# A four-layer gated cross-attention kernel: query projections two head groups at a time, with the bias added by TensorE

## The reference, cut to what matters

```python
x = x + tanh(g_xattn[l]) * xattn_l(layernorm(x), ctx)     # l = 0..3
x = x + tanh(g_ffn[l])   * ffn_l(layernorm(x))
# layer 0 and 2 (16 heads of 8): q = x@Wq + bq; k = ctx@Wk + bk; v = ctx@Wv + bv
#   out = softmax(q k^T * scale [+ mask * -1e9]) v @ Wo + bo   (mask in layer 2 only)
# layer 1 (16 heads of 8): q = x@Wq.T; k, v of concat(ctx, x) (64 + 256 keys), no biases;
#   the first key has weight tanh(gate), the softmax goes over the rest; layernorm of the result, @ Wp.T + bp
# layer 3 (8 heads of 64): plain cross-attention, then the output projection
```

## Time and profile before

| | us |
|---|---|
| median of 3 runs (lowest, highest) | 1292.36 (1283.95, 1293.24) |
| the profiled execution, whole | 1285.64 |
| its span, first to last instruction | 1283.9 |
| mean granted TensorE clock in it | 0.842 of full speed |
| busy: TensorE matmul, VectorE, ScalarE, GpSimd | 977.4, 771.4, 571.7, 393.6 |
| first DMA issue of attention 0, 1, 2, 3 | 16.82, 213.59, 815.74, 1016.87 |
| statistics' first operation of feed-forward 1, 2 (L1457) | 537.2, 957.5 |
| first DMA issue of feed-forward 0, 3 | 126.40, 1163.94 |

### The profile page before, as it was taken

The page is one execution under the profiler, slowest core; times in us unless marked ns, Lnnn a source line. Parts: engine busy times, 40 slices in busy tenths (PEclk is TensorE's granted clock), DMA queues, the critical chain, the costliest instruction groups (busy, mean ns, idle before and its releaser), DMA issues. The chain is left out here.

```text
span 1283.9 us, 17163 instructions
## 1 busy us (share of the span) xinstructions
PE 977.4 (76%) x5366; PEld 731.0 (57%) x5366; DVE 771.4 (60%) x1924; ACT 571.7 (45%) x1101; POOL 393.6 (31%) x519
## 2 busy tenths in 40 slices
PE   2797576698888888488888888478867578883766
PEld 2575354566566665266666666357745357772544
DVE  3687565566766777366666656356765414545674
ACT  1575242355555555155555544156634133321553
POOL 2432002122323232146565656333310132210321
PEclk9899677667777778689999999689978679996887
DMA  4000000000000000000000000100000200000001
GB/s 117 1 2 2 1 1 19 1 18 18 18 18 18 18 9 10 1 1 1 1 1 1 1 1 1 36 1 2 2 19 1 64 2 1 1 1 1 1 1 33
DMA packets 25607, 14.12 MB, mean 11 GB/s; under 512 B 10776, under 2 KB 25007, under 8 KB 25391
## 3 DMA queue, kind: packets, MB, share of 16 engines
q1 hardware_dynamic: 25518, 13.03, 3.8%
HBM read 11.98 MB, written 1.05 MB: 10 GB/s over the span
## 5 line engine op out<-in xcount | busy, mean ns | idle before, releaser
L1470 POOL TENSOR_TENSOR L1f_h<-L1f_h,L1f_gb 128x512 f32<-128x512 f32 (+1 forms) x96 | 152.2, 1588 | 116.5 <-DVE L1f_h L1760 96.7
L718 ACT ACTIVATE L_pt<-bank 128x512 f32<-128x512 f32 x224 | 131.3, 597 | 60.8 <-PE bank L604 56.9
L705 ACT ACTIVATE L_part<-bank,L_bias_ca,const 128x256 fp32r<-128x256 f32 x128 | 68.9, 563 | 111.9 <-PE bank L545 111.9
L406 POOL TENSOR_TENSOR L_kc<-L_kc_all,const 128x256 fp32r<-128x256 f32 x96 | 59.0, 618 | 179.7 <-PE bank L604 127.1
L1760 DVE TENSOR_TENSOR L1f_h<-L1f_a,bank 128x512 f32<-128x512 f32 (+1 forms) x96 | 65.4, 682 | 69.9 <-ACT L1f_a L1600 69.3
L1600 ACT ACTIVATE L1f_a<-bank 128x512 f32<-128x512 f32 (+1 forms) x96 | 57.3, 597 | 111.9 <-PE bank L1525 111.8
L1768 DVE TENSOR_TENSOR L1f_h_lo<-L1f_h,L1f_h_hi 128x512 fp32r<-128x512 f32 (+1 forms) x96 | 88.2, 919 | 11.1 <-ACT L1f_h_hi L1613 11.1
L844 DVE TENSOR_REDUCE L_ms<-bank 128x2 f32<-128x512 f32 x128 | 84.5, 687 | 17.0 <-PE bank L566 16.7
L566 PE MATMUL bank<-L_k,L_q 32*128 32x256 f32 x256 | 73.4, 397 | 12.2 <-DVE L_ms L844 8.9
L830 DVE SCALAR_TENSOR_TENSOR L_q<-bank,L_bias_c,L_part 128x256 fp32r<-128x256 f32 x96 | 46.2, 481 | 58.9 <-ACT L_part L705 57.7
L842 DVE TENSOR_REDUCE L_mc<-bank 128x8 f32<-128x512 f32 (+1 forms) x96 | 65.4, 682 | 24.2 <-PE bank L559 14.8
(11 more groups left out here) (405 smaller groups left out, 2608.9 us busy)
## 6 DMA issues: line engine op xcount, KB each, us to landing
L_raw<-in_L_ffn_w_dram SPq DMA_DIRECT2D x8, 176.0 KB, 2.3
L_raw<-in_L_ffn_v_dram SPq DMA_DIRECT2D x8, 176.0 KB, 2.5
const<-in_const_dram SPq DMA_DIRECT2D x1, 1036.0 KB, 5.0
x<-in_x_dram SPq DMA_DIRECT2D x2, 512.0 KB
L_raw<-in_L_ffn_w_dram SPq DMA_DIRECT2D x8, 128.0 KB, 2.6
L_mask<-in_mask_Bx1xSxS_ff_dram SPq DMA_DIRECT2D x2, 512.0 KB
out_dram<-x SPq DMA_DIRECT2D x2, 512.0 KB
L_raw<-in_L_ffn_w_dram SPq DMA_DIRECT2D x8, 48.0 KB, 2.5
```

What stands on the lines that cost most here:

```text
L705: last = act.activation(part[:, i].bitcast(F32R), b_proj[:, i * S:(i + 1) * S], ACT.Identity, bias=bias_ca[:, i, g:g + 1], scale=pr.c("ak" ...
L718: act.activation(pt[:, g // 2, (g % 2) * NS + i], b_st[(g * NS + i) % 2][:], ACT.Exp, scale=scale).then_inc(sem["exp_done"], 1)
L1470: pool.tensor_tensor(h[0:m, r], h[0:m, r], gb[0:m, gate_slot(c)], ALU.mult).then_inc(sem["h_done"], 1)
```

## The change

Six things are changed.

1. In layers 0 and 2 two groups are projected in one pass ("unit"): `proj(b, u)` makes groups 2u and 2u+1 in the two halves of one 512-column bank; there are two units per batch. ScalarE rounds 512 columns at once (Copy with a scale operand and no bias), VectorE adds 512 columns at once (tensor_tensor). In layer 1 a unit is q and k of one group, rounded by two ScalarE operations (k's scale differs, `ak1`), and added by one of VectorE.
2. The bias is added by TensorE, as the first matmul of each half: in layers 0 and 2 over two rows (`bias_q`, the rounded bias and its rest; `ones_r`), in layer 1 over one row (`neg_row`) and for k only.
3. q and k lie in one tile `qk`: in layers 0 and 2 a ring of three pairs, in layer 1 four pairs (q, k).
4. In `order`, layers 0 and 2 have a `proj` in groups 1 and 3 only, for batch b+1.
5. The bias preparation: `bias_row` and `bias_x` have two partitions, VectorE makes `bias_part` and `bias_q`, TensorE turns only the key bias (four matmuls in the code, not eight).
6. Only the first 409 columns of the constants are loaded at the start. `selc` is loaded by the attentions 0 and 2, `sum3` and `self3` by attention 3, `self0` and `self3` by the feed-forwards 0 and 3, each into a buffer that is free then, ahead of the wait for the stage's loads.

```diff
-                  ("selc", 256), ("i2", 128), ("self0", 512), ("self3", 512), ("e8", 8),
-                  ("sum3", 512)):
+                  ("ak1", 1), ("neg_row", 128), ("i2", 128), ("e8", 8),
+                  ("selc", 256), ("self0", 512), ("self3", 512), ("sum3", 512)):
...
+KEPT = CONST["selc"][0]
...
-                sp.dma_start(pr.const[:], ins["const"]).then_inc(const_in, 16)
+                sp.dma_start(pr.const[:], ins["const"][:, 0:KEPT]).then_inc(const_in, 16)
...
-        part = sb("part", [P, 2, S])
-        q = sb("q", [P, NG, S], F32R)
+        part = sb("part", [P, 2 * S])
+        qk = sb("qk", [P, NG if own_keys else 3, 2, S], F32R)
...
+        UNITS = NG if own_keys else NG // 2
+        def unit(b, g):
+            return b * UNITS + (g if own_keys else g // 2)
+        def query(b, g):
+            return (g, 0) if own_keys else (unit(b, g) % 3, g % 2)
...
-            + [s for g in (0, 1) for s in (("proj", 0, g), ("keys", 0, g))] + banks("scores", 0, 0) + [("proj", 0, 2), ("keys", 0, 2)] \
+            + [("proj", 0, u) for u in range(UNITS // 2)] + [("keys", 0, 0), ("keys", 0, 1)] + banks("scores", 0, 0) \
+            + [("proj", 0, UNITS // 2), ("keys", 0, 2)] \
...
-                for at in group(g + 3):
-                    steps += [("proj", *at), ("keys", *at)]
+                if own_keys:
+                    steps += [("proj", *at) for at in group(g + 3)]
+                elif more and g % 2:
+                    steps += [("proj", b + 1, g // 2)]
+                steps += [("keys", *at) for at in group(g + 3)]
...
+                if not gated:
+                    sp.dma_start(pt[:, 0, 0, 0:2 * P], pr.late_const("selc")).then_inc(sem["loaded"], 16)
...
-                def proj(b, g):
+                def proj(b, u):
                     pe.wait_ge(sem["xt_lo"], b + 1)
-                    need(pe, sem["qk_split"], b * NG + g)
-                    cols = slice(g * P, (g + 1) * P)
-                    for i in range(2 if own_keys else 1):
-                        o = b_proj[:, i * S:(i + 1) * S]
-                        pe.matmul(o, wx[:, 2 * i, cols], xt_hi[:], start=True, stop=False)
+                    need(pe, sem["qk_split"], b * UNITS + u)
+                    for e in range(2):
+                        g, i = (u, e) if own_keys else (2 * u + e, 0)
+                        cols = slice(g * P, (g + 1) * P)
+                        o = b_proj[:, e * S:(e + 1) * S]
+                        if biased:
+                            pe.matmul(o, bias_q[:, cols], ones_r[:], start=True, stop=False)
+                        elif i == 1:
+                            pe.matmul(o, neg_row[:], ones_r[0:1], start=True, stop=False)
+                        alone = not (biased or i == 1)
+                        pe.matmul(o, wx[:, 2 * i, cols], xt_hi[:], start=alone, stop=False)
                         pe.matmul(o, wx[:, 2 * i, cols], xt_lo[:], start=False, stop=False)
                         last = pe.matmul(o, wx[:, 2 * i + 1, cols], xt_hi[:], start=False, stop=True)
...
-                def proj(b, g):
-                    act.wait_ge(sem["proj_done"], b * NG + g + 1)
-                    need(act, sem["qk_split"], b * NG + g)
-                    for i in range(2 if own_keys else 1):
-                        last = act.activation(part[:, i].bitcast(F32R), b_proj[:, i * S:(i + 1) * S], ACT.Identity,
-                                              bias=bias_ca[:, i, g:g + 1], scale=pr.c("ak" if i else "aq"))
+                def proj(b, u):
+                    act.wait_ge(sem["proj_done"], b * UNITS + u + 1)
+                    need(act, sem["qk_split"], b * UNITS + u)
+                    if own_keys:
+                        act.activation(part[:, 0:S].bitcast(F32R), b_proj[:, 0:S], ACT.Copy, scale=pr.c("aq"))
+                        act.activation(part[:, S:].bitcast(F32R), b_proj[:, S:], ACT.Copy, scale=pr.c("ak1")).then_inc(sem["proj_hi"], 1)
+                    else:
+                        act.activation(part[:].bitcast(F32R), b_proj[:], ACT.Copy, scale=pr.c("aq")).then_inc(sem["proj_hi"], 1)
...
-                    for i in range(2 if own_keys else 1):
-                        last = dve.scalar_tensor_tensor((k if i else q)[:, g], b_proj[:, i * S:(i + 1) * S], bias_c[:, i, g:g + 1],
-                                                        part[:, i], ALU.add, ALU.add)
+                    need(dve, sem["st_done"], b * U + (u + 1) * NS - U if own_keys else (2 * b + u - 2) * 2 * NS)
+                    at_u = u if own_keys else (2 * b + u) % 3
+                    dve.tensor_tensor(qk[:, at_u].rearrange("p e s -> p (e s)"), b_proj[:], part[:], ALU.add).then_inc(sem["qk_split"], 1)
...
+                    prep(dve.tensor_scalar(bias_part[:].bitcast(F32R), bias_x[:, 0], pr.c("am")[0:2], None, ALU.mult))
+                    prep(dve.tensor_tensor(bias_q[:], bias_x[:, 0], bias_part[:], ALU.add))
...
+                sp.dma_start(sum3[:].rearrange("p c n -> p (c n)"), pr.late_const("sum3")).then_inc(sem["loaded"], 16)
+                sp.dma_start(pt[:, 0:2].rearrange("p c s -> p (c s)"), pr.late_const("self3")).then_inc(sem["loaded"], 16)
...
+                if layer in (0, 3):
+                    sp.dma_start(h[:, 0], pr.late_const(f"self{layer}")).then_inc(sem["loaded"], 16)
```

More of the change, by code:

```diff
@@ L484, in _ @@
                 if biased:
[L486 to L490, removed]
+                    pe.wait_ge(sem["prep_dve"], 6)
+                    for g in range(NG):
+                        last = pe.matmul(b_sc[1][:, g:g + 1], bias_x[0:1, 1, g * P:(g + 1) * P], ones1[0:1, 0:1],
+                                         start=True, stop=True)
                     last.then_inc(sem["prep_pe"], 1)
                 pe.wait_ge(sem["prep_dve"], DVE_WEIGHTS)
-                for g, bank in enumerate((b_st[0], b_st[1], b_mt, b_o)):
+                for g, bank in enumerate(KV):
                     cols = slice(g * P, (g + 1) * P)
@@ L558, in scores @@
                             ts = slice(t * P, (t + 1) * P)
-                            last = pe.matmul(o[:, t * S:(t + 1) * S], q[:, g, ts], kc[:, g], start=True, stop=not masked)
+                            last = pe.matmul(o[:, t * S:(t + 1) * S], qk[:, at_q, e_q, ts], kc[:, g], start=True, stop=not masked)
                             if masked:
@@ L565, in scores @@
                         for t in range(2):
-                            last = pe.matmul(o[:, t * S:(t + 1) * S], q[rows, g, t * P:(t + 1) * P], k[rows, g], start=True, stop=True)
+                            last = pe.matmul(o[:, t * S:(t + 1) * S], qk[rows, g, 0, t * P:(t + 1) * P], qk[rows, g, 1], start=True, stop=True)
                     last.then_inc(sem["sc_done"], 1)
@@ L595, in weights @@
                                 continue
-                            pe.matmul(op, keys_of, q[:, g], start=True, stop=False)
+                            pe.matmul(op, keys_of, qk[:, at_q, e_q], start=True, stop=False)
                             if masked:
@@ L603, in weights @@
                             op = o[:, kt * S:(kt + 1) * S]
-                            last = pe.matmul(op, k[rows, g, kt * P:(kt + 1) * P], mt[rows, g % 2], start=True, stop=True)
+                            last = pe.matmul(op, qk[rows, g, 1, kt * P:(kt + 1) * P], mt[rows, g % 2], start=True, stop=True)
                     last.then_inc(sem["st_done"], 1)
@@ L674, in _ @@
                 n_act = 2 if gated else 0
-                for g, bank in enumerate((b_st[0], b_st[1], b_mt, b_o)):
+                for g, bank in enumerate(KV):
                     act.wait_ge(sem["prep_pe"], pe_at + g + 1)
                     act.wait_ge(sem["prep_dve"], DVE_WEIGHTS + g)
-                    act.activation(hk.bitcast(F32R), bank[:], ACT.Identity, bias=bias_ca[:, 1, g:g + 1], scale=pr.c("ak")).then_inc(sem["prep_act"], 1)
+                    act.activation(hk.bitcast(F32R), bank[:], ACT.Identity, bias=bias_ca[:, g:g + 1], scale=pr.c("ak")).then_inc(sem["prep_act"], 1)
                 for h, bank in enumerate((b_proj, b_turn)):
@@ L1122, in sums @@
                     for c in range(NC):
-                        last = pe.matmul(b_sum[:, 0:S], pr.c("sum3")[:, c * P:(c + 1) * P], pt[:, c], start=(c == 0), stop=(c == NC - 1))
+                        last = pe.matmul(b_sum[:, 0:S], sum3[:, c], pt[:, c], start=(c == 0), stop=(c == NC - 1))
                     last.then_inc(sem["sum_done"], 1)
@@ L1388, in ffn @@
         PREP_ACT = {0: 0, 1: 0, 2: 3, 3: 0}[layer]
-        LOADED = 16 * {0: 2, 1: 2, 2: 3, 3: 2}[layer]
+        LOADED = 16 * {0: 3, 1: 2, 2: 3, 3: 3}[layer]
         def front(i):
```

89 lines of the change are left out of this document (48 added, 41 removed).

## The result

The changed kernel takes 1375.62 us (1374.3 to 1396.17, four runs) against 1288.15 (1277.4 to 1293.24) before: a ratio of 1.0687, 95% interval 1.0592 to 1.0782. It is slower, as forecast, but by 87 us and not 50; 1338 was forecast, with a range up to 1358. The profiled execution took 1376.01, its span 1374.2, which is 90.3 more than the span before. Some executions fall into a state over 1.5% slower, here the one of 1396.17: the medians have them in, the ratios leave them out.

The account below looks back on a forecast made before the run. The prediction took a chain from projection through ScalarE and VectorE to the next scores to pace layers 0 and 2, TensorE nearly full in layer 1; 17.4 + 17.4 + 4 + 12 - 2.5 + 2.2 = +50.5 us gave 1338, range 1304 to 1358.

Parts of the forecast that it names:

- The price of a bias matmul: One- or two-row matmul between 128-row ones: its block costs 0.51 us at full clock, 0.76 at half clock.
- The second rival: A bias matmul costs its columns only, 0.12 us (0.21 at half clock): +14 us, total 1300; 12%.
- Layer 0 and layer 2, one batch: Steady batches grow by 2.5 us each, +17.4 us per layer over seven batches; group 3 +1.70 on 2.05.
- third rival: Clock falls in layers 0 and 2 too, a third of both stages at half clock: +24 us, total 1361; 10%.
- The principle: Layers 0 and 2: two of four groups have the whole doubled pass on the chain; the others only lose three matmuls.
- Constants: Smaller first load -2.5 us, attention 3's first wait +2.2, feed-forwards 0; together 0, at most 2 either way.
- Layer 1: Bias block in each of 32 groups, less shorter ScalarE and VectorE operations: 1.5 us a batch, +12, ends -12 and +21.

Follow-up runs that it names:

- early pair: The changed kernel with the second pair of a batch in layers 0 and 2 projected in group 2, not group 3: 1382.0 us, ratio 1.074.
- before_l1_wide: The kernel before with only layer 1's part of the change, its bias matmul over 128 rows: 1268.9 us, ratio 0.990.
- before_zero_wide: The kernel before plus one 256-column zero-weight matmul over 128 rows in each pass of layer 1: 1284.8 us, ratio 0.999.
- before_zero_one_row: The kernel before plus one 256-column zero-weight matmul over one row in each pass of layer 1: 1334.7 us, ratio 1.041.
- before_pv_last: The kernel before with layer 1's products with v put behind the weights and scores, not between them: 1322.9 us, ratio 1.030.

## Why the prediction was wrong in size

Step by step:

- **The price of a bias matmul** (0.51 and 0.76): right, 0.51 and 0.82. The second rival (its columns only) is out for few rows, and true for 128 rows.
- **Layer 0 and layer 2, one batch** (+2.5): right, 12.17 against 9.53 and, for the batches at full clock, 15.06 against 12.58. Group 3 came within 0.01. The two stages took 24 us each instead of 19.4: in layer 0 the first two batches grew by 3.2 and 4.0 (the second had a clock of 0.73 where it had 1.00), in layer 2 some batches took 16.59 at 0.90. That is the third rival in small: at most 9.5 us together, of the 24 that it was given.
- **The principle** (half as many passes are no half chain): right for group 3. But most of what the pair costs is no wait for q: of the 2.13 us that group 3 lost in the early pair, 1.63 came back in group 2, where nobody waits for it. It is the place of its eight matmuls in TensorE's order, which the sum had priced (1.38 of 1.70) and the principle does not name.
- **Constants**: -1.8 for -2.5; in attention 3 the first wait is now 8.6 us, not 6.23, and the stage +2.1 for +2.2. The feed-forwards, put at 0, took 8.3 us less together. 3.9 of it are feed-forward 2, which the change leaves alone: 63.9 us at a clock of 0.74 before, 60.0 at 0.81 after. It takes 60.5 at 0.81 in before_l1_wide too, and 63.8 in before_zero_wide, so this is the spread from one execution to another and no gain of the change. The other three took 1.1 to 2.0 less each, down to 85.9, 281.9 and 117.9, and take 84.9, 281.5 and 116.8 in before_zero_one_row, which leaves them alone.
- **Layer 1** (1.5 us a batch, +12, "ends: -12 and +21"): this step failed. It priced the block at either clock and took the mix of the two clocks as given. The runs show that the mix is what the change moves. The block at a like clock is worth little: the best batch of after took 36.45 us at 0.75, the like one before 35.55 at 0.78, 0.9 more. The mean went from 36.17 at 0.73 to 41.04 at 0.62, 4.9 a batch, and the stage gained 50. Its upper end of 21 was no bound, since it too kept the clock.

The third rival had the mechanism but put it into layers 0 and 2, where the earlier trace rows shows 1.00 and 0.99. What fell was the clock that stood between its two levels already: 0.73 in layer 1. With layer 1 at the forecast +12 the span would have grown by 52, close to the forecast 50.5. That closeness has luck in it: layers 0 and 2 took 9.5 more than forecast, and the feed-forwards 8.3 less.

What was shown of the cause: one added matmul over one row in each pass of layer 1 is enough to bring its clock down, in either kernel, over 32 rows it does the same (tried in the changed one), and over 128 rows it is harmless. Layer 1 ran at 1.2 and at 2.4 GHz by turns before, and a mean clock that falls is more of its time at 1.2. By what means the matmul does that was not shown. The Trainium skill, TensorE: Matmul & The Clock Gate, A second HAM failure mode: psum-queue depth-cycling, describes a kernel in which short idle moments of TensorE between groups of matmuls make the granted clock oscillate. By that reading, the runs agree in part: the pauses around a change of rows seem to have the larger share. But pauses are not all: before_pv_last has 20 us more of waits in its stretch and its clock is 0.70, while the gaps around the one-row matmul are 0.4 to 0.6 us in each of 20 passes, 8 to 12 us, and the clock is 0.57. Since before_pv_last has fewer changes of rows too, it doesn't separate the two. Why narrow streaming adds to it stays open as well.

## What to carry to other kernels

Among matmuls over 128 rows a small one is cheap only if it has 128 rows too: pad a one-row bias with zeros to 128 rows and it costs its columns (0.12 us here), leave it at one or two and it costs 0.5, and far more where the clock is already between its levels (50 us for 32 of them). Among 32-row matmuls a 32-row one had no gaps, but 32 of them still cost 16 us in that stage. A forecast should treat the mean granted clock of such a stage as a result of the change, with its own two ends (the stage at 1.2 GHz throughout, and at 2.4). And grouping two passes of a chain into one saved instructions here and no time: not with the first reader right behind it (10.80 us a batch with the cheap bias, against 9.54), and not with a whole group between them (10.37).

## What was not expected of the hardware

- 32 added matmuls of 0.5 us each (0.8 at half clock) lowered layer 1's granted clock from 0.73 to 0.57 and cost 50 us in all, two to three times what they last.
- A matmul over 32 rows is no better than one over one row (1376.5 and 1375.6 us for the whole).
- Shorter operations on ScalarE and VectorE, with a 128-row bias matmul, raised the clock of the same stage from 0.73 to 0.81 and made five batches 11.7 us shorter, though TensorE had one more matmul in each pass (one profiled execution of each).
